# Weighted sum's strips and small loads issued in the stage before, and its preparations on VectorE put between the strips

## The chip, the cores and the metric

One core of a Trainium2 chip runs the whole program in a single launch. The metric is device time in microseconds, the median of several runs; the lower the better. The kernel before takes 2534.42 us (three runs, 2531.26 to 2535.39).

## What is computed

A chain of graph layers over 3125 nodes with 96 features and 50000 edges that are sorted by target, each wrapped as `layernorm(x + layer(x))`:

```python
x = _layernorm(x + _L0_gnn_ref(x, edge_index))        # 16 steps of normalised neighbour sums
x = _layernorm(x + _L1_gnn_ref(x, W0, b0, ..., src, dst))   # 2 layers: neighbour sum, weights, x / std
x = _layernorm(x + _L2_gnn_ref(x, edge_index, edge_weight)) # weighted neighbour sum
x = _layernorm(x + _L3_gnn_ref(x, edge_index, edge_attr_32, ...)) # 2 convolutions with a maximum over edges

def _L2_gnn_ref(X, edge_index, edge_weight):
    dst, src = (edge_index[0], edge_index[1])
    messages = edge_weight[:, None] * X[src]
    out = jax.ops.segment_sum(messages, dst, num_segments=X.shape[0])
    return out
```

## The kernel before

The nodes are padded to 25 blocks of 128 (`NB` = 25, `NP` = 3200), and a node block is a tile of 128 x 96. The program runs seven stages in a row, each a block of five instruction streams with a barrier of all engines behind it (`stage`): `prepare` and `build_counts` make a 3200 x 3200 matrix of edge counts `at` in float16 in SBUF; `appnp` multiplies by it 16 times and meanwhile GpSimd adds the edge weights into a matrix in HBM (`weight_matrix`, `d.mt`); `sage` does two more products by the counts with small weights and norms; `weighted_sum` is the third layer; `edge_conv` runs twice.

`weighted_sum` (tag `l2`) is the stage around which the change is made. The weight matrix has 25 strips, one for each block of targets; a strip is 128 x 27 x 128 float32, 1728 KB, of which 25 blocks meet node blocks and 2 meet "carried" rows: rows of `x` that a partition shares with another and that are fetched by two indirect DMAs on GpSimd (`far`) from a copy of `x` in HBM (`d.xt`, `x_table`). A matmul takes float16, so each strip and `x` are split into a high and a low part. In the kernel before, the engines' queues are these, in the order written:

- SyncE: strip 0, the store of `x` to `x_table` (lines 1196 and 1198), then strips 1 to 24. There are four places for strips (`STRIPS_IN`), so strip `o` waits until the low half of strip `o - 4` is made by VectorE (and by GpSimd, from `POOL_FROM` = 1 on).
- ScalarE: 17 small loads (targets, sources by tile, weights, biases, sources; lines 1349 to 1357), the high parts of `x` (1359), then for each strip its high half (1368); behind strip 0's, the high part of the carried rows (1371); a root behind strip 3's.
- GpSimd: waits for `x_table`, two gathers of the carried rows (1212), then the low half of the last 6 of 27 blocks (`BY_POOL`) of each strip from 1 on (1220).
- VectorE: the low parts of `x` (1231), the sources by tile (1298, 1299), the squares of the weights (`square_weights`), what depends on the targets (`edge_ends`, 1248 to 1265), the carried rows' low part, and then for each strip its low half (1310), with `bound_scales` behind strip 2, the carry row and `stream_of` behind 3, two scales behind 4, `stream_of` behind 5, and each five strips' sums, norm and table parts.
- TensorE: for each strip 54 matmuls with the high half and 54 with the low one (1395), into one half of a bank; strip 0's first pass waits group by group for the low parts of `x`, the last group being the carried rows. Behind strip 0 come the column norms (1413, 1414), behind strip 2 the carry row (1419).

The stage before it, `sage`, ends with the last group of five blocks: ScalarE's root (`square_root`, 157), VectorE's deviation and second norm (980 to 1041), a second root, and the last product with the inverse root into `m.x` (1060). Four other groups of that last norm are finished by ScalarE (947). SyncE has only the loads of the layer's weights there, at the start; GpSimd has one reduction over the partitions between the two layers. In `appnp`, VectorE starts with the scaled `dinv` (728), from which the first parts are made.

## Time and profile before

| what | value |
|---|---|
| median of 3 runs | 2534.42 us |
| the profiled execution's own time | 2547.56 us |
| its span, first to last instruction | 2545.8 us |
| TensorE matmul / VectorE / ScalarE / GpSimd busy | 81% / 67% / 36% / 49% of the span |
| `weighted_sum` from and to (us of the span) | 1368.8 to 1541.0 |
| last big product of `sage` ends; first gather of `edge_conv` issued | 1350.4; 1555.76 |
| mean granted clock of TensorE | 0.905 of full speed |

The profile is one execution. Times in the trace count from its first instruction. Shares of busy time are means over seven stages with different limits, so a reading for one stage takes the timeline of each engine in it, the waits with what ended them, and a table of busy time by stretch. In a timeline, "[idle before <- releaser]" is the time that the engine stood before the instruction and what ended it; neighbours of the same kind are merged ("x50" is fifty of them, from the start of the first to the end of the last). SP is SyncE, PE TensorE, DVE VectorE, ACT ScalarE, POOL GpSimd; "SPq", "ACTq" are DMAs that those engines issue.

### The profile page before, as it was taken

The page shows a single profiled execution, that of the slowest core. Times are in us where ns is not written, and L with a number is a line of the kernel's source. Part 1 is how long each engine was busy: PE and PEld are TensorE (multiplying, and loading weights), DVE is VectorE, ACT ScalarE, POOL GpSimd, SP SyncE. Part 2 cuts the span into 40 slices and gives each one's busy share as a digit, 9 for nine tenths or more (in the row PEclk, how much of TensorE's full clock was granted, in tenths as well). Part 3 has the DMA queues.
Part 4 walks back from the last instruction along what each step waited for, and adds up shares of the span by engine and source line. Part 5 has one row for each costly group of instructions (what it writes and reads, how often), then busy time and mean ns, then how long its engine had stood idle before and what let it go on. Part 6 is the DMA issues. An engine that isn't in the chain of part 4 may idle for free. (4 is left out here: it accounts for less than half of the span.)

```text
span 2545.8 us, 59620 instructions
## 1 busy us (share of the span) xinstructions
PE 2058.7 (81%) x23672; PEld 1897.4 (75%) x23672; DVE 1715.1 (67%) x4704; ACT 913.5 (36%) x1320; POOL 1249.8 (49%) x1021
## 2 busy tenths in 40 slices
PE   4494569999999999997983897888887578888860
PEld 4242259999999999997883896777776567778760
DVE  8999985555555555566555995767775356776656
ACT  0395520000000000001344555766773156777620
POOL 0200048878787778750001543666665246666651
PEclk9995579999999999998996997999998589999975
DMA  3593013232323232220004862344333034334321
GB/s 131 166 408 139 1 15 30 21 30 21 30 21 27 24 30 21 21 30 14 2 2 166 319 264 72 121 131 133 113 114 116 16 98 136 115 119 130 126 75 27
DMA packets 150636, 227.45 MB, mean 89 GB/s; under 512 B 87617, under 2 KB 109793, under 8 KB 147074
## 3 DMA queue, kind: packets, MB, share of 16 engines
q1 hardware_dynamic: 70418, 186.31, 20.2%
q0 software_dynamic: 74688, 28.51, 11.6%
q10 hardware_dynamic: 5296, 9.47, 1.2%
q8 instruction: 152, 2.49, 0.4%
q14 instruction: 82, 0.67, 0.1%
HBM read 123.37 MB, written 100.84 MB: 88 GB/s over the span
## 5 line engine op out<-in xcount | busy, mean ns | idle before, releaser
L637 PE MATMUL ps<-parts,at 128*128 128x192 f16 x11250 | 942.8, 247 | 23.7 <-POOL at L669 13.8
L637 PEld LDWEIGHTS ps<-parts,at 128*128 128x128 f16 x11250 | 935.8, 98 | 25.3 <-issue 24.3
L1782 PE MATMUL ps<-yparts,source_onehots_c 128*128 128x192 f16 x7000 | 681.3, 251 | 119.4 <-issue 103.5
L1782 PEld LDWEIGHTS ps<-yparts,source_onehots_c 128*128 128x128 f16 x7000 | 581.5, 100 | 185.5 <-issue 166.7
L1574 POOL DMA_INDIRECT messages_c<-y_table,srci_sb x504 | 499.6, 991 | 384.5 <-PE ps L1782 140.1
L679 POOL DMA_INDIRECT weight_matrix<-w,place x392 | 608.4, 1552 | 157.7 <-issue 96.5
L767 DVE SCALAR_TENSOR_TENSOR t<-ps,coef,g 128x96 f32<-128x96 f32 x400 | 126.8, 317 | 245.3 <-PE ps L637 202.3
L707 ACT ACTIVATE ea_limbs<-ea_in,ea_scale 128x392 f16<-128x392 f32 x32 | 19.9, 621 | 742.7 <-DMA ea_in<-in_eaT 734.4
L1657 DVE TENSOR_SCALAR source_onehots_c<-sources_spread,shift 128x1280 f16<-128x1280 f16 x512 | 283.1, 563 | 0.3
L1602 ACT ACTIVATE source_gaps_c<-sources_spread,unshift 128x1280 f16<-128x1280 f16 x188 | 256.3, 1364 | 23.0 <-DVE source_onehots_c L1657 5.5
L1706 DVE SCALAR_TENSOR_TENSOR messages_c<-messages_c,brk 128x96 f32<-128x96 f32 x784 | 249.9, 319 | 17.3
L1605 ACT ACTIVATE source_onehots_c<-source_gaps_c 128x1280 f16<-128x1280 f16 x188 | 238.8, 1270 | 6.0
L627 PE MATMUL ps<-onekey,oneplace 128*128 128x200 f16 x784 | 154.9, 358 | 80.5 <-DVE oneplace L582 80.5
L627 PEld LDWEIGHTS ps<-onekey,oneplace 128*128 128x128 f16 x784 | 78.9, 122 | 156.4 <-DVE oneplace L582 108.0
L1685 DVE TENSOR_TENSOR messages_c<-messages_c,ps 128x480 f32<-128x480 f32 x112 | 67.0, 598 | 149.4 <-remote 126.4
L1614 ACT ACTIVATE picked_pairs_c<-ps 128x384 f32<-128x384 f32 x140 | 59.7, 490 | 239.3 <-PE ps L1809 220.1
L770 DVE SCALAR_TENSOR_TENSOR t<-ps,coef,t 128x96 f32<-128x96 f32 x400 | 127.3, 318 | 14.1
L777 DVE CAST parts<-t 128x96 f16<-128x96 f32 x375 | 93.9, 251 | 55.6 <-DVE t L770 1.5
L669 POOL TENSOR_TENSOR at<-at,ident 128x128 f16<-128x128 f16 x25 | 10.9, 477 | 244.8 <-issue 244.8
L1677 DVE TENSOR_TENSOR messages_c<-picked_pairs_c 128x192 f32<-128x192 f32 x140 | 49.3, 352 | 95.3 <-ACT picked_pairs_c L1614 65.1
L562 ACT ACTIVATE counts<-ps 128x400 f16<-128x400 f32 x196 | 85.9, 622 | 69.0 <-PE ps L627 65.1
L779 DVE TENSOR_TENSOR parts<-t,parts 128x96 f16<-128x96 f32 x375 | 97.8, 261 | 13.4 <-DVE parts L777 0.5
(385 smaller groups left out, 1869.0 us busy)
## 6 DMA issues: line engine op xcount, KB each, us to landing
weight_matrix<-blank SPq DMA_DIRECT2D x27, 1600.0 KB
weights<-weight_matrix SPq DMA_DIRECT2D x25, 1728.0 KB
run_max<-messages_c SPq DMA_DIRECT2D x28, 960.0 KB
ea_c<-edge_limbs SPq DMA_DIRECT2D x28, 896.0 KB
edge_limbs<-ea_limbs SPq DMA_DIRECT2D x128, 98.0 KB
run_max<-messages_c SPq DMA_DIRECT2D x28, 384.0 KB
sources_spread<-sources_by_tile ACTq DMA_DIRECT2D x26, 320.0 KB
messages_c<-y_table,srci_sb POOLq DMA_INDIRECT x504
```

The lines of the kernel that those rows point to most:

```text
L627: nc.tensor.matmul(m.ps[:, n % 8, 256 * (s % 2):256 * (s % 2) + KEYS], oneplace[:, q % RING, h, :, j], onekey[:, q % RING, h, :, j], start ...
L637: mm = nc.tensor.matmul(m.ps[:, bank, 0:2 * D], m.at[:, s, blk * P:(blk + 1) * P], parts[:, s, :], start=(s == 0), stop=(s == NB - 1))
L679: nc.gpsimd.indirect_dma_start(cells, bass.IndirectOffsetOnAxis(m.place[:, t:t + 1], 0), m.w[:, t:t + 1], None, compute_op=ALU.add).then_i ...
L767: nc.vector.scalar_tensor_tensor(t1[:, r % 2, :], m.ps[:, r % NBK, 0:D], coef[:, i:i + 1], g0[:, i, :], ALU.mult, ALU.add).then_inc(tmp1, 1)
L770: nc.vector.scalar_tensor_tensor(t2[:, r % 2, :], m.ps[:, r % NBK, D:2 * D], coef[:, i:i + 1], t1[:, r % 2, :], ALU.mult, ALU.add).then_in ...
L779: nc.vector.tensor_tensor(parts[:, nxt, i, D:2 * D], t2[:, r % 2, :], parts[:, nxt, i, 0:D], ALU.subtract).then_inc(ready, 1)
L1574: nc.gpsimd.indirect_dma_start(msg[:, k % 2, j, :], None, d.yt, bass.IndirectOffsetOnAxis(m.srci[:, k * TURN + j:k * TURN + j + 1], 0)).th ...
L1602: nc.scalar.activation(gap[:], srcb[:, k % 2, :, :].rearrange("p i e -> p (i e)"), ACT.Abs, bias=m.unshift[:, b:b + 1]).then_inc(gapd, 1)
L1605: nc.scalar.activation(hot[:, b, :], gap[:], ACT.Relu, bias=1.0, scale=-1.0).then_inc(hota, 1)
L1657: nc.vector.tensor_scalar(hot[:, b, :], srcb[:, k % 2, :, :].rearrange("p i e -> p (i e)"), m.shift[:, b:b + 1], None, ALU.is_equal).then_ ...
L1706: nc.vector.scalar_tensor_tensor(msg[:, k % 2, j, :], prev, m.brk[:, TURN * k + j:TURN * k + j + 1], msg[:, k % 2, j, :], ALU.add, ALU.max ...
L1782: return nc.tensor.matmul(m.ps[:, i // 2, at:at + 2 * D], hot[:, b, i * P:(i + 1) * P], parts[:, b, :], start=(b == 0 and i % 2 == 0), sto ...
```

## The change

The buffers of the strips (`m.strips`), of their high halves and of two small loads are now placed by hand over the counts matrix `at` (`placed`), which is free after the last big product of `sage`; so are all tensors of the later stages. With that:

- `sage`, SyncE: once the last product is done, issues strips 0 and 1, the small loads, and strip 2 (`AHEAD` = 3). ScalarE: behind the first root of the last group, stores the first 20 blocks of `x` to `x_table` and makes the high halves of strips 0 and 1; behind the second root, waits for the last norm on VectorE (`xn`) and stores the last 5 blocks. GpSimd adds `rowptr` and `deg` (`e_end`).
- `weighted_sum`, ScalarE: no loads; the high parts of `x`, the carried rows' high part, and high halves from strip 2 on; its root moves behind strip 4. GpSimd: gathers, then the low half of 6 blocks of every strip, 0 too. VectorE: strip 0's low half comes right behind the low parts of `x`; `square_weights` and the carried rows' low part behind strip 0; the sources by tile behind 1, `edge_ends` behind 2, and the four other preparations each one strip later than before. SyncE: strips from 3 on. TensorE: strip 0 runs the 25 node blocks with the high and then with the low half, and the carried rows' 2 blocks last; column norms behind strip 1, carry row behind strip 3.
- `build_counts`, GpSimd: makes the square of `dinv` and the scaled `dinv`, which VectorE made in `appnp`.

```diff
@@ build_counts, GpSimd
             nc.gpsimd.memset(m.at[:, :, NW * W:NP], 0.0).then_inc(cleared, 1)
+            nc.gpsimd.tensor_tensor(m.dinv2[:], m.dinv[:], m.dinv[:], ALU.mult).then_inc(squared, 1)
+            nc.gpsimd.tensor_tensor(m.dinvs[:], m.dinv[:], m.gs[:].to_broadcast([P, NB]), ALU.mult).then_inc(squared, 1)
             g.wait_ge(cleared, 1)
+            g.wait_ge(squared, 2)
@@ appnp, VectorE
-            do(nc.vector.tensor_scalar(dinvs[:], m.dinv[:], m.gs[:], None, ALU.mult))
...
-            do(nc.vector.tensor_tensor(coef[:], m.dinv[:], m.dinv[:], ALU.mult))
-            do(nc.vector.tensor_scalar(coef[:], coef[:], 1.0 - ALPHA, None, ALU.mult))
+            do(nc.vector.tensor_scalar(coef[:], m.dinv2[:], 1.0 - ALPHA, None, ALU.mult))
@@ sage, SyncE
             sp.wait_ge(wl, 14 * 16)
+            strips = d.mt.rearrange("(o p k c) -> p o k c", p=P, k=MB, c=P)
+            sp.wait_ge(prod, 2 * NB)
+            for o in range(2):
+                sp.dma_start(m.strips[:, o, :, :], strips[:, o, :, :]).then_inc(m.fetched[o], 16)
+            sp.dma_start(m.srcti[:], d.src_t.rearrange("t e -> (t e)").rearrange("(p c) -> p c", p=P)).then_inc(m.stl, 16)
+            sp.dma_start(m.dsti[:], d.dst_s).then_inc(m.eld, 16)
+            for k in range(2):
+                sp.dma_start(m.wmr[:, k, 0:D], d.Wmsg[k]).then_inc(m.wld, 16)
+                sp.dma_start(m.wmr[:, k, D:2 * D], d.Wroot[k]).then_inc(m.wld, 16)
+                for l in range(LIMBS):
+                    sp.dma_start(m.we[l * DE:(l + 1) * DE, k, :], d.Wedge[k]).then_inc(m.wld, 16)
+                sp.dma_start(m.bias[:, k, :], d.bias[k].rearrange("(a f) -> a f", a=1).to_broadcast([P, D])).then_inc(m.wld, 16)
+            sp.dma_start(m.srci[:], d.src_s).then_inc(m.wld, 16)
+            for o in range(2, AHEAD):
+                sp.dma_start(m.strips[:, o, :, :], strips[:, o, :, :]).then_inc(m.fetched[o], 16)
@@ sage, GpSimd
             nc.gpsimd.partition_all_reduce(ga[:], gm[:], P, RMAX).then_inc(amx, 1)
+            nc.gpsimd.tensor_tensor(m.e_end[:], m.rowptr[:], m.deg[:], ALU.add).then_inc(past, 1)
+            g.wait_ge(past, 1)
@@ sage, ScalarE
+            def strip_high(o):
+
+                a.wait_ge(m.fetched[o], 16)
+                nc.scalar.activation(m.whi[:, o, :, :], m.strips[:, o, :, :], ACT.Copy).then_inc(m.high, 1)
+
+            def store_x(g, z):
+
+                if z < NEND:
+                    a.wait_ge(xs, z)
+                else:
+                    a.wait_ge(xn, 1)
+                rows = slice(g * ENDS, z * ENDS)
+                a.dma_start(d.xt.rearrange("(i p) f -> p i f", p=P)[:, rows, :], m.x[:, rows, :]).then_inc(m.xst, 16)
...
                         square_root(nc, a, m, roots + (g if layer == 0 else 2 * g) + 1, m.st2[:], ends(g))
+                        if layer == 1:
+                            store_x(0, g)
+                            strip_high(0)
+                            strip_high(1)
...
                         square_root(nc, a, m, roots + 2 * g + 2, m.st2[:], ends(g))
+                        store_x(g, NEND)
@@ weighted_sum, SyncE
-            for o in range(NB):
+            for o in range(AHEAD, NB):
                 if o >= STRIPS_IN:
                     sp.wait_ge(low_v, o - STRIPS_IN + 1)
-                    if o - STRIPS_IN >= POOL_FROM:
-                        sp.wait_ge(low_g, o - STRIPS_IN - POOL_FROM + 1)
+                    sp.wait_ge(low_g, o - STRIPS_IN + 1)
                 sp.dma_start(mt[:, o % STRIPS_IN, :, :], strips[:, o, :, :]).then_inc(fetched[o % STRIPS_IN], 16)
-                if o == 0:
-                    sp.dma_start(d.xt.rearrange("(i p) f -> p i f", p=P), m.x[:]).then_inc(xst, 16)
@@ weighted_sum, GpSimd
+            g.wait_ge(xst, 32)
             for q in range(PARTS):
                 nc.gpsimd.indirect_dma_start(far[:, q, :], None, d.xt,
                                              bass.IndirectOffsetOnAxis(m.carried[:, q:q + 1], 0)).then_inc(farg, 16)
+            for o in range(NB):
+                low_half(o)
             g.wait_ge(farg, 16 * PARTS)
@@ weighted_sum, VectorE
             for g in range(NEND):
                 low_parts(g)
-            v.wait_ge(stl, 16)
-            do(nc.vector.tensor_copy(srcf[:], srcti[:]))
-            nc.vector.tensor_scalar(srct[:], srcf[:], -float(MID), None, ALU.add).then_inc(stm, 1)
-            square_weights()
-            edge_ends()
-            low_parts(NEND)
...
+                if o == 0:
+                    square_weights()
+                    low_parts(NEND)
+                if o == 1:
+                    v.wait_ge(stl, 16)
+                    do(nc.vector.tensor_copy(srcf[:], srcti[:]))
+                    nc.vector.tensor_scalar(srct[:], srcf[:], -float(MID), None, ALU.add).then_inc(stm, 1)
                 if o == 2:
+                    edge_ends()
+                if o == 3:
                     bound_scales()
@@ weighted_sum, ScalarE
-            a.dma_start(dsti[:], d.dst_s).then_inc(eld, 16)
...
-            a.dma_start(m.srci[:], d.src_s).then_inc(wl, 16)
             for g in range(NEND):
                 nc.scalar.activation(xp[:, blocks(g), 0:D], m.x[:, blocks(g), :], ACT.Copy, scale=XSCALE).then_inc(xhigh, 1)
-            for o in range(NB + rows_at + 1):
+            a.wait_ge(farg, 16 * PARTS)
+            nc.scalar.activation(xp[:, NB:MB, 0:D], far[:], ACT.Copy, scale=XSCALE).then_inc(xhigh, 1)
+            for o in range(2, NB + rows_at + 1):
@@ weighted_sum, TensorE
+                if o == 0:
+                    sum_blocks(o, whi, nodes, True, False)
+                    low_made(o)
+                    sum_blocks(o, wlo, nodes, False, False)
+                    pe.wait_ge(xlow, NEND + 1)
+                    sum_blocks(o, whi, carried, False, False).then_inc(highs_used, 1)
+                    sum_blocks(o, wlo, carried, False, True).then_inc(summed, 1)
```

## Rows read from the trace of the kernel before

**Rows 1.** The timeline of VectorE around the stage boundary at 1368.8 us.

```profile
1367.07 0.66 DVE L1060 TENSOR_TENSOR x_sb<-y_sb,st 128x480 f32<-128x480 f32 x1
1378.61 2.93 DVE L1231 SCALAR_TENSOR_TENSOR x_parts<-x_sb,x_parts 128x480 f16<-128x480 f32 x5 [10.88 <-ACT x_parts L1359]
...
1381.84 0.37 DVE L1299 TENSOR_SCALAR srct<-srcf 128x392 f16<-128x392 f32 x1
...
1383.78 0.35 DVE L1248 CAST dstf<-dsti 128x392 f32<-128x392 int32 x1
...
1386.64 0.18 DVE L1259 TENSOR_TENSOR e_end<-rowptr,deg 128x25 f32<-128x25 f32 x1
...
1387.99 0.18 DVE L1265 TENSOR_SCALAR unshift<-shift 128x25 f32<-128x25 f32 x1
1391.83 0.36 DVE L1231 SCALAR_TENSOR_TENSOR x_parts<-carried_x,x_parts 128x192 f16<-128x192 f32 x1 [3.66 <-ACT x_parts L1371]
...
1435.69 0.70 DVE L1330 SCALAR_TENSOR_TENSOR y_sb<-ps,weight_unscale,x_sb 128x480 f32<-128x480 f32 x1
```

**Rows 2.** The timeline of ScalarE in the same stretch.

```profile
1359.97 0.21 ACT L157 ACTIVATE sd<-st 128x5 f32<-128x5 f32 x1 [2.31 <-DVE st L985]
1365.80 0.21 ACT L157 ACTIVATE sd<-st 128x5 f32<-128x5 f32 x1 [5.62 <-DVE st L1041]
1368.81 0.39 ACTq L1349 DMA_DIRECT2D dsti<-in_dst_s  x1
...
1377.97 2.58 ACT L1359 ACTIVATE x_parts<-x_sb 128x480 f16<-128x480 f32 x5 [11.96 <-issue]
...
1391.36 0.36 ACT L1371 ACTIVATE x_parts<-carried_x 128x192 f16<-128x192 f32 x1 [7.84 <-DMA carried_x<-x_table,carried]
...
1425.61 3.08 ACT L1368 ACTIVATE weights_high<-weights 128x3456 f16<-128x3456 f32 x1 [3.84 <-DMA weights<-weight_matrix]
```

**Rows 3.** The timeline of TensorE in the same stretch.

```profile
1383.57 4.18 PE L1395 MATMUL ps<-x_parts,weights_high 128*128 128x96 f16 x50 [27.90 <-ACT weights_high L1368]
...
1401.05 2.47 PE L1395 MATMUL ps<-x_parts,weights_high 128*128 128x96 f16 x54
...
1443.31 4.04 PE L1395 MATMUL ps<-x_parts,weights_low 128*128 128x96 f16 x54 [2.45 <-DVE weights_low L1310]
```

**Rows 4.** The timeline of GpSimd, the first gather of the carried rows.

```profile
1383.67 1.25 POOL L1212 DMA_INDIRECT carried_x<-x_table,carried  x1 [109.80 <-DMA x_table<-x_sb]
```

**Rows 5.** Busy time by stretch: length, PE, PEld, DVE, ACT, POOL, PEclk, DMA share, GB/s.

```profile
1401.00:1420.00 19.00, 18.00 (x415) 17.80 (x415) 17.95 (x32) 10.49 (x5) 11.45 (x5) 1.00 0.85 306
1440.00:1460.00 20.00, 17.19 (x357) 16.88 (x353) 19.58 (x13) 12.36 (x6) 10.37 (x3) 0.91 0.91 342
```

**Rows 6.** Durations by line: count, then ns at least/median/most.

```profile
L1310 DVE TENSOR_TENSOR weights_low<-weights,weights_high x25: 2943/2957/4404, 1392.1 to 1521.7; 128x2688 f16<-128x2688 f32 x24, 128x3456 f16<-128x3456 f32 x1
...
L1574 POOL DMA_INDIRECT messages_c<-y_table,srci_sb x504: 938/946/1579, 1555.8 to 2447.2; - x168
```

**Rows 7.** The timeline of VectorE at the head of `appnp`.

```profile
340.52 0.24 DVE L728 TENSOR_SCALAR dinv_scaled<-dinv,g_scale 128x25 f32<-128x25 f32 x1 [0.76 <-PEq L101]
```

**Rows 8.** The timeline of SyncE, two strips' issues (start, duration).

```profile
1369.66 10.28 SPq L1196 DMA_DIRECT2D weights<-weight_matrix  x1
...
1418.52 0.32 SPq L1196 DMA_DIRECT2D weights<-weight_matrix  x1
```

**Rows 9.** DMA issues at the span's end; us from issue to landing.

```profile
out<-x_sb SPq DMA_DIRECT2D x5, 240.0 KB, 2.3
```

**Rows 10.** DMA queues from 1372.0 to 1375.5 us: packets, MB, share of 16 engines.

```profile
q1 hardware_dynamic: 84, 1.13, 86.2%
q10 hardware_dynamic: 87, 0.14, 10.7%
```

**Rows 11.** Bytes moved from 1555.5 to 1562 us in 40 slices.

```profile
GB/s 32 0 0 0 0 0 0 0 0 0 0 0 0 19 151 132 0 0 0 0 0 0 95 208 0 0 0 0 0 0 189 114 0 0 0 0 0 0 227 76
```

**Rows 12.** Groups of VectorE by line and shape, 1392 to 1530 us.

```profile
L1310 DVE TENSOR_TENSOR weights_low<-weights,weights_high 128x3456 f16<-128x3456 f32 x1 | 3.8, 3752 | 0.0
```

156 lines of the change are left out of this document (85 added, 71 removed).

## The prediction

> **What bounds the kernel now.** I read the change first and asked which stages it touches: the end of layer two of `sage` (its last norms), the whole of `weighted_sum`, and two small operations at the head of `appnp`. So the page's shares for the whole span say little here; I went to the engine timelines on both sides of the stage boundary at 1368.8 us, and then to the table of stretches. In the boundary the reader should see this order: VectorE ends the last norm at 1367.07+0.66 = 1367.73 us [rows 1]; the next stage's first instruction comes 1.08 us later, and it is ScalarE's list of 17 small loads, which holds ScalarE until 1377.97 [rows 2]. TensorE waits until 1383.57 for its first matmul, runs 50 of strip 0's in 4.18 us, and starts strip 1 only at 1401.05, where 54 take 2.47 [rows 3]. What it waits for in between are the carried rows: `x_table` is stored, gathered from 1383.67 on [rows 4], and ScalarE gets them at 1391.36 [rows 2]. That is the wait the change aims at.
>
> Then I asked which engine sets the pace once strips flow, because only that engine's lead can be kept. From 1401 to 1420 VectorE is busy 17.95 of 19.00 us, from 1440 to 1460 19.58 of 20.00; TensorE 18.00 and 17.19 [rows 5]. VectorE is the one without slack: a strip's low half takes it 2.96 us as a rule and up to 4.40 [rows 6], and norms and bounds stand between them in the same queue. So from 1392 to the end of the strips I read VectorE's queue as the path, and I measure the change at one point of that queue: the moment at which the carried rows' low part (line 1231, at 1391.83 [rows 1]) is made.
>
> **Part 1, the head of `appnp`.** VectorE loses `dinv_scaled`, 0.24 us with a 0.03 gap [rows 7], ahead of all that makes the first parts: 0.27 us gained. The square of `dinv` comes off the queue when TensorE already has parts to work on; I take nothing. GpSimd gets both in `build_counts`, where it has a single memset and then nothing to do until the stage ends: no cost, since no engine waits for them before the stage ends.
>
> **Part 2, the last norms.** SyncE issues strips 0 and 1, the 17 small loads and strip 2, from the last big product (about 1350.4) on. A list of 17 took ScalarE 9.16 us (1368.81 to 1377.97 [rows 2]), so SyncE is through by about 1361, before the norms are: it is no late comer at the boundary. A strip issued alone took from 1418.52 [rows 8] to 1425.61, where ScalarE had waited for it [rows 2]: 7.1 us. So strip 0 is there by 1357.6 and strip 1, about 4.5 behind, by 1362. ScalarE's first root of the last group ends at 1359.97+0.21 = 1360.18; then it issues the store of 20 blocks (0.4) and copies two strips, 3.08 each [rows 2]: 1366.75. Its second root stood at 1365.80 [rows 2] and is now 0.95 late; the chain on VectorE behind it ends at 1368.7. ScalarE then issues the store of the last five blocks, 0.43, which VectorE's end formerly didn't have to wait for. With the same 1.08 for the boundary, the next stage begins at 1370.2: **1.4 us are lost**, and everything below is counted from there.
>
> **Part 3, the first strips.** ScalarE starts at once with the high parts of `x` instead of its list. VectorE follows: five low parts end 3.57 us after ScalarE's start (1377.97 to 1378.61+2.93 [rows 1, 2]), then strip 0's low half 2.95, then the squares of the weights, about 1: it stands at the carried rows at 1377.7. Up to here nothing binds but VectorE itself.
>
> When are the carried rows there? Call their arrival F; before it was 1391.36. It is the time at which the second part of the store has landed plus the gather. The store: 240 KB alone took 2.3 us to landing [rows 9], which from 1368.7 gives 1371.0. But two queues share the DMA engines packet for packet: beside strip 0 the one queue had 84 packets and the other 87 in the same 3.5 us [rows 10], while the bytes were 1.13 against 0.14 MB. The store has 25 x 128 = 3200 short rows, a strip only 128 long ones, so beside strips the store nearly stands still. It gets on between strips 1 and 2 and after strip 2; if the rest isn't through when strip 3 (issued at 1370.2) comes, it ends behind it, at about 1370.2+7.1+0.8 = 1378.1. I take 1375.5, past the middle, since the row with two queues at once is nearer to the case than the store alone. The gather: from 1383.67 to 1391.36 it took 7.7 us under full DMA traffic [rows 2, 4]; in a quiet stretch the first bytes of one flow 2 us after its issue ([rows 11]: slices of 0.16 us from 1555.5 on, and the issue was at 1555.76), which with a second gather 1.55 behind and its landing is about 5. Behind strip 3 the engines are quiet, because strip 4 must wait for GpSimd's share of strip 0, which is queued behind the gathers: I take 6.4. **F = 1381.9**, between 1376.0 and 1385.8.
>
> So at this point VectorE's queue is 1391.36-1381.9 = 9.46 us early. What it must do behind the point has changed. Gone is strip 0's low half, 3.75 [rows 12]. Added are the two operations on the sources (the second at 1381.84 for 0.37 [rows 1], the two 0.75) and `edge_ends`, 1383.78 to 1388.17, 4.39, less 0.22 for its addition [rows 1]: in the kernel before all of this lay in the wait for the carried rows, cover that is gone. Net +1.17. GpSimd takes 6 of 27 blocks of strip 0 while VectorE is idle, so it costs nothing; strip 2's high half waits for F on ScalarE and is made by F+3.4, while VectorE wants it at F+4.5.
>
> Who is late next? TensorE: strip 1 can begin at about 1384.4 and it needs less than 4.9 us a strip (two halves of 2.47 that overlap [rows 3]), where the strips so far came at 5.6 (strip 1 at 1401.05, strip 8's low half at 1443.31 [rows 3]); it keeps its slack. Strips 4 on are issued as VectorE frees the buffers, 7.1 to landing against three strips' lead. So VectorE stays the bound, and at the end of the strips the lead is the same; the tail behind and both `edge_conv` are untouched.
>
> Sum: 9.46-1.17+0.27 = 8.56 us. The profiled execution took 2547.56 us (its span 2545.8), which would become 2539.0; it is 13.1 above the median of the runs, and no term is a share of the span, so I take the same off the median: 2534.42-8.56 = **2525.9**.
>
> **The rivals.**
> *TensorE's lead is kept whole (0.07).* It starts strip 1 at 1384.4 instead of 1401.05, 16.6 us; if VectorE's busy time holds slack, since some of its low halves last 4.40 instead of 2.96 us where it only waits for GpSimd [rows 6], the time is 2534.4-16.6-0.3 = 2517.5. Against: 19.58 of 20.00, and a wait inside an instruction is spent all the same.
> *The store is through before strip 3 (0.06).* F near 1377.7, where VectorE itself is the limit: 13.7-0.9 = 12.8, 2521.6.
> *The carried rows come late (0.15).* Store 1378.1 and the full 7.7: F = 1385.8, gain 4.7, 2529.7.
> *VectorE shuts GpSimd's gathers out (0.08).* GpSimd's additions do wait while VectorE has two operands in SBUF. If gathers did too, they would start when strip 0's low half ends, at 1376.7, not 1375.5: F = 1383.1, gain 7.4, 2527.0. Against: 504 gathers beside a busy VectorE took 938 to 1579 ns [rows 6]. The Trainium skill (SBUF — State Buffer, "SBUF: two separate sides") says that the pair of ports is an exclusive lock and that a DMA issued from GpSimd starves meanwhile, as its descriptors can't be written. By that rule it is this rival that holds; the trace so far doesn't bear it out for gathers, only for additions.
> *An issue blocks (0.08).* SyncE's strip behind the long store of `x_table` took 10.28 us to issue [rows 8]. If ScalarE's second store stands so behind its first, the boundary moves by some 6 us, and with it everything: about 2.5 gained, 2531.9.
> *Slower: TensorE's clock (0.06).* Between strips 2 and 3 there is now `edge_ends`, 4.4 us on VectorE beside the low half's 2.96, and the bounds follow strip by strip, so TensorE waits some 2.5 us in each of about five strips. After a wait of 2.45 us a half strip took 4.04 us, not 2.47 (at 1443.31 [rows 3]; the granted clock is 0.91 in that stretch and 1.00 in 1401 to 1420 [rows 5], so it was at the lower level, 1.2 GHz, for part of it). A strip with both halves so costs some 8.1 us against the pace of 5.6: 2.5 lost each. The mechanism decides from 6 strips on, since 8.6+5.1 us must go; with nine, 22.5 are lost and the time is 2548. Against: a TensorE that is late has no waits, and the clock came back each time it was busy throughout.
>
> **How the numbers follow.** The forecast has 0.50. What a measurement of this kernel can tell from no change is about 0.2%, 5.1 us, so faster means below 2529.35. Faster: nearly all of the forecast, the first two rivals, most of the shut-out gathers and a third of the late rows: 0.73. Same: most of the late rows, the blocked issue: 0.20. Slower: the clock and a remainder, 0.07. The range takes in F from 1376 to 1385.8 and the blocked issue, and stops short of the whole of TensorE's lead: 2519.5 to 2532.5; outside it are about 0.06 below and 0.08 above.
>
> **What the changed profile would show.** Next stage's first instruction near 1370.2; ScalarE's second root of the last group near 1366.8; the carried rows' copy on ScalarE near 1381.9 with VectorE waiting for it since 1377.7; strip 1 on TensorE near 1384.4; the first sums of five strips on VectorE (1435.7 before) near 1427.5. If the carried rows are early and those sums aren't, VectorE's queue grew more than I counted. If the sums are earlier by over 12 us, VectorE was not the bound. If the boundary is later than 1372, an issue or a strip stood in ScalarE's way.

## The result

The changed kernel takes 2524.07 us (median of 5 runs, 2521.57 to 2525.85) against 2533.16 of the kernel before in the same series: ratio 0.9969, 95% interval 0.9958 to 0.9980, so 5 to 11 us faster. The forecast was 2525.9 with 73% on faster. The number is right, but it is the sum of three terms of which none was forecast with its size: a loss of 7.1 us was taken for nothing, and two gains were put too low. That the sum came out is luck. (In the first series of experiments below every run, those of before too, took near 2350 us instead of 2530, all of it in `edge_conv`, so a kernel is compared only by its ratio to the runs of before in its own series.) The ledger of the two profiled executions (before's took 2547.56 us, after's 2525.85, span 2524.1):

| stretch | forecast | measured |
|---|---|---|
| `build_counts`, to VectorE's last memset: 339.61 before, 346.75 after | 0 | +7.1 |
| from there to the last matmul of `sage`: 1015.5, then 1013.7 | -0.3 | -1.8 |
| from there to VectorE's first operation of `edge_conv`: 186.6, then 174.1 | -8.3 | -12.4 |
| sum up to `edge_conv` | -8.6 | -7.1 |

Behind that, `edge_conv` is the same work in both; that it was 14.6 us shorter in this execution is not the change's, as the medians differ by 9.1 us in all. The 2 us between these 9.1 and the 7.1 of the ledger are within the interval; the tiles of `edge_conv` lie elsewhere now, and whether that does anything stays open.

**Build.** Busy time by stretch (length, PE, PEld, DVE, ACT, POOL, PEclk, DMA share, GB/s), before and then after, while the weight matrix is cleared:

```profile
110.00:160.00 50.00, 50.00 (x263) 24.47 (x262) 50.00 (x67) 50.00 (x132) 0.00 (x0) 1.00 1.03 408
```

```profile
110.00:160.00 50.00, 50.00 (x262) 24.33 (x260) 50.00 (x67) 50.00 (x131) 49.65 (x1) 1.00 1.02 385
```

GpSimd is "busy" for the whole stretch with one 128x25 operation: it stood 53.60 us, beside VectorE's one-hots, which follow each other without a gap (they still did when it ended, so what let it in is not shown). More to the point, the clearing moves 385 GB/s, not 408, and so lasts until about 219 us, not 212 (by the bytes of the stretch from 200 to 220 us). VectorE's additions behind the one-hots stop where registers are loaded, and longer while the clearing runs; these waits in the build (waited for: us, times, longest), before and after, and the loads of registers from 180 to 210 us (ns at least/median/most):

```profile
DVE at L606 <- issue: 6.0, 13, 1.0
...
L600 DVEq TENSOR_LOAD <-off_sb x8: 1117/1136/1439, 179.9 to 204.1; - x8
```

```profile
DVE at L624 <- issue: 12.0, 13, 2.6
...
L618 DVEq TENSOR_LOAD <-off_sb x8: 1983/2007/2219, 179.8 to 209.5; - x8
```

The median load takes 1.13 to 1.15 us there in all nine traces with the quick clearing and 1.97 to 2.01 in all five with the slow one; behind the clearing it takes 0.60 in each.

**Head of `appnp`.** GpSimd's 25 additions and TensorE's first matmuls, before:

```profile
347.73 10.94 POOL L669 TENSOR_TENSOR at<-at,ident 128x128 f16<-128x128 f16 x25 [244.82 <-issue]
348.25 11.92 PE L637 MATMUL ps<-parts,at 128*128 128x192 f16 x123 [13.78 <-POOL at L669]
```

and after, where the stage begins at 347.65:

```profile
347.64 15.10 POOL L687 TENSOR_TENSOR at<-at,ident 128x128 f16<-128x128 f16 x25 [182.75 <-POOLq L101]
350.32 0.96 PE L655 MATMUL ps<-parts,at 128*128 128x192 f16 x5 [8.71 <-DVE parts L754]
```

Before, GpSimd's first addition comes 7.2 us behind VectorE's first operation; now both begin at once, share, and TensorE's first matmul comes 2.7 us into the stage, not 7.7. What GpSimd waited for is in its sequencer's rows, of before and then of after:

```profile
L669 POOLq MODIFY_POOL_CONFIG  x2: 11/11/11, 340.6 to 340.6; - x2
```

```profile
L553 POOLq MODIFY_POOL_CONFIG  x2: 12/12/12, 102.7 to 102.8; - x2
110.36 53.60 POOL L553 TENSOR_TENSOR dinv_squared<-dinv 128x25 f32<-128x25 f32 x1 [7.63 <-issue]
```

GpSimd's configuration is changed ahead of the first operation on two tensors (`TENSOR_TENSOR`) that follows its reduction over the partitions, and in all 14 traces that operation begins 6.9 to 7.6 us after this first change. In before the change of configuration stands at the head of `appnp`, where TensorE waits for it. With the two operations in the build, it is paid there, where nothing waits for GpSimd.

**Boundary.** ScalarE of after (start, duration; compare [rows 2]):

```profile
1364.83 0.21 ACT L172 ACTIVATE sd<-st 128x5 f32<-128x5 f32 x1 [2.31 <-DVE st L1038]
1364.84 0.44 ACTq L945 DMA_DIRECT2D x_table<-x_sb  x1
1365.32 6.06 ACT L936 ACTIVATE weights_high<-weights 128x3456 f16<-128x3456 f32 x2 [0.28 <-issue]
1371.29 0.19 ACT L172 ACTIVATE sd<-st 128x5 f32<-128x5 f32 x1
1373.29 0.37 ACTq L945 DMA_DIRECT2D x_table<-x_sb  x1
1374.70 2.58 ACT L1403 ACTIVATE x_parts<-x_sb 128x480 f16<-128x480 f32 x5 [3.22 <-PEq L101]
1385.04 0.36 ACT L1405 ACTIVATE x_parts<-carried_x 128x192 f16<-128x192 f32 x1 [7.76 <-DMA carried_x<-x_table,carried]
```

VectorE and GpSimd of after (compare [rows 1, 4]):

```profile
1378.19 2.95 DVE L1354 TENSOR_TENSOR weights_low<-weights,weights_high 128x2688 f16<-128x2688 f32 x1
...
1385.43 1.50 DVE L1283 SCALAR_TENSOR_TENSOR x_parts<-carried_x,x_parts 128x192 f16<-128x192 f32 x1 [3.44 <-ACT x_parts L1405]
1386.86 2.95 DVE L1354 TENSOR_TENSOR weights_low<-weights,weights_high 128x2688 f16<-128x2688 f32 x1
1389.72 1.81 DVE L1361 CAST srcf<-srcti 128x392 f32<-128x392 int32 x1
...
1428.87 0.71 DVE L1383 SCALAR_TENSOR_TENSOR y_sb<-ps,weight_unscale,x_sb 128x480 f32<-128x480 f32 x1
```

```profile
1379.19 3.01 POOL L1269 DMA_INDIRECT carried_x<-x_table,carried  x1 [93.61 <-DMA x_table<-x_sb]
1382.50 0.95 POOL L1269 DMA_INDIRECT carried_x<-x_table,carried  x1 [0.30 <-issue]
```

The first gather took 3.01 us, not 1.25, and it ends 1.06 behind VectorE's low half (1381.14): it was held for as long as that ran. TensorE of after (compare [rows 3]):

```profile
1376.14 4.16 PE L1436 MATMUL ps<-x_parts,weights_high 128*128 128x96 f16 x50 [15.07 <-DVE x_parts L1283]
1385.26 3.74 PE L1436 MATMUL ps<-x_parts,weights_low 128*128 128x96 f16 x50 [4.96 <-POOL weights_low L1264]
...
1389.17 2.46 PE L1436 MATMUL ps<-x_parts,weights_high 128*128 128x96 f16 x54
...
1404.18 3.41 PE L1436 MATMUL ps<-x_parts,weights_low 128*128 128x96 f16 x54 [2.20 <-DVE weights_low L1354]
```

From the last matmul of `sage` on (1355.09 before, 1360.43 after), the stage begins 14.2 us later instead of 13.7, the carried rows' low part comes at 25.0 instead of 36.7, the first sums of five strips at 68.4 instead of 80.6, `edge_conv` at 174.1 instead of 186.6. All that is gained is there by the first sums.

### The profile page after: what moved, and what is told of

Its sections match the earlier page's. It is cut to its first block and busy times, and to the rows that moved or that the text cites. A ratio compares the mean times of both kernels' runs of the same rounds, so it can differ in the third digit from the quotient of the medians.

```text
span 2524.1 us, 59625 instructions
## 1 busy us (share of the span) xinstructions
PE 2057.6 (82%) x23672; PEld 1883.9 (75%) x23672; DVE 1708.9 (68%) x4701; ACT 914.6 (36%) x1320; POOL 1308.8 (52%) x1025
## 5 line engine op out<-in xcount | busy, mean ns | idle before, releaser
L1835 PEld LDWEIGHTS ps<-yparts,source_onehots_c 128*128 128x128 f16 x7000 | 566.1, 98 | 189.9 <-issue 165.2
L687 POOL TENSOR_TENSOR at<-at,ident 128x128 f16<-128x128 f16 x25 | 15.1, 640 | 182.7 <-POOLq L101 182.7
L795 DVE TENSOR_TENSOR parts<-t,parts 128x96 f16<-128x96 f32 x375 | 97.2, 259 | 13.4 <-DVE parts L793 0.5
```

Of the source, the lines that this page charges most:

```text
L795: nc.vector.tensor_tensor(parts[:, nxt, i, D:2 * D], t2[:, r % 2, :], parts[:, nxt, i, 0:D], ALU.subtract).then_inc(ready, 1)
L1835: return nc.tensor.matmul(m.ps[:, i // 2, at:at + 2 * D], hot[:, b, i * P:(i + 1) * P], parts[:, b, :], start=(b == 0 and i % 2 == 0), sto ...
```

## The experiments

Twelve kernels, in three series of four. Each series has its own runs of the kernel before beside it, and only ratios to those are compared. The two stages around the change are alike in all series. The table reads the traces: GB/s of the clearing (110 to 160 us) and the build's last memset; then, in us from ScalarE's first copy in `weighted_sum`, the first gather and how long its issue took, the carried rows on ScalarE, their low part on VectorE, and the first sums; then the us from the last matmul of `sage` to the first operation of `edge_conv`.

| kernel | GB/s | build ends | gather (us) | rows | low part | sums | to `edge_conv` | ratio |
|---|---|---|---|---|---|---|---|---|
| before | 408 | 339.6 | 5.7 (1.25) | 13.4 | 13.9 | 57.7 | 186.6 | 1 |
| after | 385 | 346.8 | 4.5 (3.01) | 10.3 | 10.7 | 54.2 | 174.1 | 0.9969 |
| `build_alone` | 409 | 339.4 | 6.9 (1.19) | 14.2 | 14.7 | 58.7 | 187.6 | 0.9998 |
| `build_undone` | 385 | 346.3 | 4.5 (3.04) | 10.3 | 10.7 | 54.2 | 174.2 | 0.9977 |
| `ends_in_wait` | 385 | 346.7 | 4.6 (3.10) | 10.6 | 16.9 | 54.5 | 173.9 | 0.9963 |
| `store_first` | 385 | 346.6 | 4.5 (2.96) | 11.9 | 12.3 | 54.6 | 174.6 | 0.9967 |
| `before_blank` | 385 | 346.8 | 5.8 (1.20) | 13.8 | 14.3 | 58.2 | 188.3 | 1.0027 |
| `blank_moved` | 409 | 339.6 | 4.5 (3.05) | 10.4 | 10.8 | 54.2 | 174.4 | 0.9934 |
| `ends_first` | 408 | 339.3 | 4.7 (1.19) | 8.9 | 17.0 | 54.3 | 173.4 | 0.9941 |
| `vector_alone` | 409 | 339.6 | 6.0 (2.26) | 14.9 | 15.3 | 56.8 | 174.4 | 0.9943 |
| `alone_ends` | 408 | 339.6 | 8.9 (1.19) | 14.7 | 15.1 | 52.8 | 170.9 | 0.9931 |
| `rows_first` | 409 | 339.5 | 7.2 (2.26) | 12.6 | 13.0 | 49.6 | 167.2 | 0.9922 |
| `store_whole` | 409 | 339.4 | 10.8 (1.19) | 14.8 | 15.2 | 58.7 | 176.8 | 0.9953 |
| `strips_back` | 408 | 339.6 | 1.2 (1.19) | 10.4 | 17.1 | 59.9 | 179.6 | 0.9967 |

(In before, `build_alone` and `before_blank` that first copy stands behind 9 us of loads, so their columns in between start later.) The intervals of the ratios are 0.0010 to 0.0014 to each side.

**`build_alone`**: the first part of the change alone, made in the kernel before.

```diff
 # before, build_counts, GpSimd
+            nc.gpsimd.tensor_tensor(m.dinv2[:], m.dinv[:], m.dinv[:], ALU.mult).then_inc(squared, 1)
+            nc.gpsimd.tensor_tensor(m.dinvs[:], m.dinv[:], m.gs[:].to_broadcast([P, NB]), ALU.mult).then_inc(squared, 1)
```

> The kernel before with GpSimd's two additions in the build alone (the square of dinv and dinv_scaled on GpSimd in build_counts, both off VectorE in appnp). Nothing is left out. In the profile of after, the build ended 7.1 us later than in that of before (346.75 against 339.61), GpSimd's 128x25 operation stood for 53.60 us, and the zeroing of the weight matrix moved 385 GB/s, not 409. Theory (the operations cost nothing, the 7.1 us are the zeroing's rate in that one execution): this kernel takes 2532.9, the time of before less 0.3, and its build is long or short as its own zeroing is slow (385) or quick (409). Rival (GpSimd's held operation disturbs the zeroing or VectorE): +7, 2540, with about 385 GB/s and a build of 245 us between its first and last memset.

Ratio 0.9998 (0.9988 to 1.0008), with GpSimd's operation as long as in after and the clearing at full rate:

```profile
110.00:160.00 50.00, 50.00 (x263) 24.33 (x262) 50.00 (x67) 50.00 (x131) 50.00 (x1) 1.00 1.03 409
```

The held operation disturbs nothing. But the theory is only half right: it put the 7 us down to one slow execution.

**`build_undone`**: the same two operations taken out of the changed kernel.

```diff
 # after, build_counts, GpSimd
-            nc.gpsimd.tensor_tensor(m.dinv2[:], m.dinv[:], m.dinv[:], ALU.mult).then_inc(squared, 1)
-            nc.gpsimd.tensor_tensor(m.dinvs[:], m.dinv[:], m.gs[:].to_broadcast([P, NB]), ALU.mult).then_inc(squared, 1)
```

> The changed kernel with the two operations back on VectorE at the head of appnp, so that only the last norms and the first strips differ from before. Nothing is left out. Theory (they cost nothing in the build and give 0.3 at the head of appnp): 2524.4. Rival (the held operation costs 7 us in the build): 2517. What is then between this kernel and before is the worth of the strips' part alone: by the trace of after, from the last big product of sage to the first operation of edge_conv 174.1 us instead of 186.6, so 12.4 less, where the forecast had 8.3.

Ratio 0.9977 (0.9968 to 0.9985), 5.4 us of 2352. The build ended at 346.28 with 385 GB/s although the operations were gone. So the 7 us belong to the change and not to its GpSimd operations: something that all kernels made from after share. Its head of `appnp` is before's again, TensorE waiting for GpSimd's additions:

```profile
354.88 11.30 PE L652 MATMUL ps<-parts,at 128*128 128x192 f16 x102 [13.76 <-POOL at L684]
```

From the build's end to the last matmul of `sage` the three traces without the two operations on GpSimd take 1015.5, 1016.4 and 1017.0 us, the eleven with them 1013.6 to 1015.6, 1014.6 in the mean: about 1.7 us for the head, where 0.27 was forecast. It is all there at the end of `appnp`'s first product: VectorE's 25th combination of sums begins 62.0 to 63.1 us behind the build's last memset in the three, 59.7 to 61.1 in the eleven. Runs alone don't resolve it. Nor does a run take VectorE's 0.24 us away and leave GpSimd's change of configuration where it was; but that change, at 347.2 here, and the 7.1 us behind it are all of GpSimd's wait.

**`ends_in_wait`**: what VectorE does behind strips 1 and 2 put into its wait for the carried rows.

```diff
 # weighted_sum, VectorE, o == 0
                     square_weights()
+                    (the two operations on the sources)
+                    edge_ends()
                     low_parts(NEND)
```

> The changed kernel with the two operations on the sources and edge_ends in front of the carried rows' low part instead of behind strips 1 and 2. Nothing is left out. In the trace of after VectorE waits 3.44 us there for the carried rows and is busy without a gap from 1385.43 to 1443.31. Theory (VectorE's queue is the bound of the first strips): the wait is filled, the first sums of five strips come 3.4 us nearer to the stage's start (54.2 us after ScalarE's first copy in after, then 50.8), the time falls by 3.4 to 2520.7. Rival (TensorE or the transfers set the pace of the first strips): the sums stay at 54.2, 2524.1. Third (VectorE's work shuts GpSimd's gathers out: in after the first of them took 3.01 us and ended as VectorE's low half of strip 0 did): the carried rows come up to 5 us later and the time is that of after or up to 2 more.

Ratio 0.9963 (0.9951 to 0.9976); the sums came at 54.5, as the second and third theories had it, and neither's reason is in the trace. The rows came at 10.6, so nothing shut them out for longer; TensorE had waits left. VectorE lost the gain itself:

```profile
1385.77 3.94 DVE L1302 TENSOR_TENSOR brk<-dstf 128x391 f32<-128x391 f32 x1
...
1391.10 1.62 DVE L1311 TENSOR_SCALAR row_ends<-row_ends 128x25 f32<-128x25 f32 x1
```

These take 0.57 and 0.17 us when nothing is beside them. GpSimd's low halves of strips 0 and 1 ran from 1386.04 to 1389.28.

**`store_first`**: strip 3 asked for behind the store.

```diff
 # weighted_sum, SyncE, ahead of strip 3
+                if o == AHEAD:
+                    sp.wait_ge(xst, 32)
```

> The changed kernel with strip 3 asked for only when both parts of the store of x_table have landed. Nothing is left out. Theory (strip and store share the DMA engines packet for packet, so strip 3 at 1374.67 holds up the store issued at 1373.29, which had landed by 1379.2): the store lands 2.3 to 3 us after its issue, the gathers are issued before VectorE's low half of strip 0 begins (3.5 us after the stage's start), the carried rows are on ScalarE near 6.5 us after the stage's start instead of 10.3, VectorE's wait of 3.44 us is gone, 2520.7. Rival (what holds the carried rows is VectorE's low half, which shuts the gathers out, and the store was through in time): carried rows and time as in after, 2524.1; strip 3 comes 1 to 2 us later for nothing.

Ratio 0.9967 (0.9955 to 0.9979). The store took no less time to land: the second part was issued at 1375.02 and SyncE went on at 1380.78, 5.8 us later, where 5.6 had gone in after with strip 3 beside it. What the store waits for is strip 2. Packets by queue (q1 SyncE's strips, q10 ScalarE's store) from 1373 to 1377 us, while strip 2 moves, and from 1377 to 1381:

```profile
q1 hardware_dynamic: 150, 1.60, 94.0%
q10 hardware_dynamic: 277, 0.11, 9.5%
...
q10 hardware_dynamic: 1347, 0.51, 46.9%
q1 hardware_dynamic: 26, 0.14, 8.3%
```

So the theory's mechanism holds, with the wrong strip; and strip 3, now beside the gathers, brought the rows 1.6 us later (11.9), which moved the sums by 0.4.

**`before_blank`** and **`blank_moved`**: what do all kernels made from after share? Three new tiles (`row_ends`, `dinv_squared`, `dinv_scaled`), each taking 128 bytes per partition, are allocated ahead of all that follows, so `blank`, the source of the clearing, begins at byte 202176 instead of 201792. (`build_alone` has two of them: 202048.) Both kernels are made by the same two lines, in before and in after:

```diff
 # build_counts
+        sb("pad_ahead", [P, 32], F32)
         blank = sb("blank", [P, NP // 4], F32)
+        sb("pad_behind", [P, 32], F32)
```

> The kernel before with 128 unused bytes per partition in front of blank (the zeros from which the weight matrix is cleared in the build) and 128 behind it. blank then begins at byte 201920 of each partition, not 201792; the other tiles of the build move by 256. Nothing is left out. Seen so far: the clearing moved 409 GB/s in before and build_alone (blank at 201792 and 202048, both 64 bytes past a multiple of 256) and 385 in after and the three kernels made from it (202176, 192 past one), and the build was 7 us longer in these, with or without GpSimd's two operations. Theory (where blank begins sets the rate): 385 GB/s, the build's last memset near 346.5 instead of 339.5, 7 us slower than before, ratio 1.003. Rival (something else of the change, such as where other tiles or the program's instructions lie): 409 GB/s and the time of before.

> The changed kernel with the same 128 bytes in front of blank and 128 behind it: blank begins at 202304, 64 past a multiple of 256 as in before. Nothing is left out. Theory: 409 GB/s, the build ends near 339.5, 7 us less than after; on a chip where after stands to before as 0.997, this stands as 0.994. Rival: 385 GB/s and the ratio of after, 0.997.

Ratios 1.0027 (1.0016 to 1.0039) and 0.9934 (0.9921 to 0.9948): 128 unused bytes ahead of `blank` (and 128 behind, which keep the later tiles in step) make before 7 us slower and the changed kernel some 9 faster, 7 by the trace. `before_blank` and then `blank_moved`:

```profile
110.00:160.00 50.00, 50.00 (x263) 24.49 (x262) 50.00 (x67) 50.00 (x132) 0.00 (x0) 1.00 1.02 385
```

```profile
110.00:160.00 50.00, 50.00 (x263) 24.46 (x262) 50.00 (x67) 50.00 (x132) 50.00 (x1) 1.00 1.03 409
```

The starts 201792, 202048 and 202304, each 64 bytes past a multiple of 256, gave 408 or 409 GB/s in every trace; 201920 and 202176, each 192 past one, gave 385. The Trainium skill (DMA: Bandwidth & Descriptors, "How a descriptor splits into AXI transactions") says that a descriptor is cut at multiples of 256 bytes and that a first piece is fetched from the boundary below its start. In the trace of before the clearing's packets have the 3200 bytes that `blank` has per partition (6572 packets with 20.38 MB from 110 to 160 us, 204 of them tiny). By that account the good start needs 13 pieces and the bad one 14, which gives an estimate of 0.93 for the ratio of the rates; counted in the beats of 32 bytes that the same section has, the unused ones included, it is 102 against 106, or 0.96. The traces have 0.94, between the two, so they agree in kind and don't tell which count sets the rate. A start on a multiple of 256 would need 13 pieces too; no run tried it.

**`ends_first`**: on `blank_moved`, the moved work even further ahead.

```diff
 # weighted_sum, VectorE
             for g in range(NEND):
                 low_parts(g)
+            (the two operations on the sources)
+            edge_ends()
             stepped = 0
```

> blank_moved with the two operations on the sources and edge_ends behind the low parts of x and in front of strip 0's low half, not behind strips 1 and 2. Nothing is left out. Where these stood in the wait behind strip 0's low half (ends_in_wait), GpSimd's low halves came at the same time: edge_ends took 9.0 us instead of 6.4 and the first sums were not earlier. Theory (VectorE's queue is the bound, and the gathers are shut out only by long operations on two operands): here nothing of GpSimd's is due beside edge_ends, so it takes 4.4 us, the gathers are issued in 1.25 and 0.95 us, the carried rows' low part comes 1.6 us later than in after and 8.6 us are gone behind it: first sums 7 us, less a stall or two of 1.2, nearer to the stage's start than in after (54.2), about 48.4; time 5 to 6 below blank_moved. Rival (TensorE or the strips' transfers set the pace once VectorE is early): first sums at 52 or later, time within 2 of blank_moved.

Ratio 0.9941 (0.9927 to 0.9954). What it says of the gathers holds: with no long operation on VectorE beside them they took 1.19 and 0.95, and the rows came at 8.9 instead of 10.4.

```profile
1372.58 1.19 POOL L1271 DMA_INDIRECT carried_x<-x_table,carried  x1 [93.58 <-DMA x_table<-x_sb]
1374.07 0.95 POOL L1271 DMA_INDIRECT carried_x<-x_table,carried  x1 [0.30 <-issue]
1375.04 3.23 POOL L1266 TENSOR_TENSOR weights_low<-weights,weights_high 128x768 f16<-128x768 f32 x2
```

But "nothing of GpSimd's is due beside `edge_ends`" was wrong, since early gathers let GpSimd go on to its low halves at 1375.04, and one operation of 0.27 us stood for both of them:

```profile
1374.74 3.61 DVE L1311 TENSOR_SCALAR mrep<-ones,mcol 128x96 f32<-128x96 f32 x1
```

The sums stayed at 54.3: from ScalarE's first copy on VectorE was idle for 4.3 us instead of 6.4, and held for 10.1 instead of 7.9 (what its operations took beyond the least that the same ones take in these traces).

**`vector_alone`**: is it GpSimd's low halves that hold VectorE?

```diff
-BY_POOL, AHEAD = 6, 3
+BY_POOL, AHEAD = 0, 3
```

(with GpSimd's low halves and the waits for them gone)

> blank_moved with the low halves of all 27 blocks on VectorE and none on GpSimd. Nothing is left out. One of 27 blocks took VectorE 3.75 us in before, one of 21 takes 2.95. Theory (a low half on GpSimd holds VectorE's two-operand work up, and the operations of 0.15 to 0.4 us that took 1.3 to 1.8 are such holds: 19 us in all behind the carried rows in after): 25 x 0.8 = 20 us are added and 19 saved, the time stays within 3 us of blank_moved, and no small operation on VectorE is stretched. Rival (GpSimd's share is free): 20 us slower than blank_moved.

Ratio 0.9943 (0.9929 to 0.9956), the time of `blank_moved` and far from 20 us slower. The holds are gone: seven low halves behind the carried rows took

```profile
L1345 DVE TENSOR_TENSOR weights_low<-weights,weights_high 128x3456 f16<-128x3456 f32 x7 | 26.3, 3756 | 0.1
```

and no small operation is stretched. So GpSimd's 6 of 27 blocks buy nothing here: a strip's share takes 0.8 us off VectorE and mostly costs it a hold of 1.2 to 1.5. What `vector_alone` lost again is in its wait for the carried rows, 7.22 us: strip 4, which no longer waits for GpSimd, was asked for between the gathers.

**`alone_ends`** and **`rows_first`**: the same two steps without GpSimd in the way.

```diff
 # vector_alone + ends_in_wait's edit; rows_first also, SyncE:
+                    if o == STRIPS_IN:
+                        sp.wait_ge(farg, 16 * PARTS)
```

> vector_alone (all low halves on VectorE) with the two operations on the sources and edge_ends in front of the carried rows' low part. Nothing is left out. In vector_alone VectorE waits 7.22 us for the carried rows and nothing of GpSimd's holds it; what is moved is 5.1 us. Theory (VectorE's queue is the bound of the first strips, and in ends_in_wait and ends_first it was GpSimd's low halves that ate the gain): the wait shrinks to 2.1, the first sums come 5.1 us nearer to ScalarE's first copy (56.8 in vector_alone, then 51.7), the time falls by 5 (0.2%) against vector_alone: ratio to before 0.992. Rival (TensorE or the transfers set the pace once VectorE is early): the sums come at 55 or later, ratio 0.994 as in blank_moved, ends_first and vector_alone.

> alone_ends with strip 4 asked for only when the carried rows have been gathered. Nothing is left out. In vector_alone SyncE asked for strip 4 as soon as VectorE had made strip 0's low half, between the two gathers, and the carried rows reached ScalarE 14.9 us after its first copy; in ends_first, without a strip beside the gathers, 8.9. Theory: the rows come 3 to 4 us earlier, at 11 to 12, VectorE's remaining wait of 2 us is gone, first sums near 50, ratio 0.991. Rival (the late strip 4 is missed later): sums as in alone_ends or later, TensorE waits for strip 4's high part.

The sums came at 52.8 (51.7 expected) and 49.6 (50 expected): now moved work does fill the wait. VectorE at the carried rows in `vector_alone` and in `rows_first`:

```profile
1383.57 0.36 DVE L1274 SCALAR_TENSOR_TENSOR x_parts<-carried_x,x_parts 128x192 f16<-128x192 f32 x1 [7.22 <-ACT x_parts L1396]
```

```profile
1382.14 0.36 DVE L1276 SCALAR_TENSOR_TENSOR x_parts<-carried_x,x_parts 128x192 f16<-128x192 f32 x1 [0.16 <-ACT x_parts L1396]
```

This settles that VectorE's queue is the bound of the first strips. Ratios 0.9931 (0.9918 to 0.9945) and 0.9922 (0.9909 to 0.9936): `rows_first`, 2512.97 us against 2531.87 of before, is the fastest kernel of all. Its trace is 7.2 us shorter than that of `blank_moved` up to `edge_conv`, the ratios differ by 3 us; the intervals allow for it, and whether some is lost in `edge_conv` stays open. So does why the store lands 1.5 to 4.4 us later in the three kernels without GpSimd's share (gather at 6.0, 8.9 and 7.2).

**`store_whole`** and **`strips_back`**: which part of the change gains? Both on `blank_moved`.

```diff
 # store_whole: sage, ScalarE
-                            store_x(0, g)
...
-                        store_x(g, NEND)
+                        store_x(0, NEND)
 # strips_back: no strip in sage
-BY_POOL, AHEAD = 6, 3
+BY_POOL, AHEAD = 6, 0
-                            strip_high(0)
-                            strip_high(1)
```

> blank_moved with x_table stored in one piece behind the last norm, not 20 blocks before the two strips' copies and 5 behind. Nothing is left out. The records of store_first show the 2560 short rows of the first part mixed one to one with strip 2's long ones and some 700 of them still waiting when strip 2 is through; the last of all leave near 1378.9, 1.9 before SyncE sees the landing. Theory (the carried rows' arrival hangs on the 3200 rows of the store): all 3200 rows now go beside strip 3, the gathers are issued 5 to 8 us later, VectorE's wait for the carried rows grows from 3.5 to 9 or 11, the first sums come 6 to 7 us later than in blank_moved (54.2), ratio 0.996. Rival (VectorE's queue has slack behind): the rows come late, the sums and the time don't, 0.9935.

> blank_moved with no strip asked for or copied in sage: strips 0 to 3 are asked for at the start of weighted_sum, strip 0's high half is made behind the high parts of x. The small loads and the store in two parts stay in sage. Nothing is left out. Theory (the gain is the carried rows', the strips ahead only fill the time until then): the second root of the last norms is 0.6 earlier, strip 0 lands 7.1 after the stage's start, its high half is made by 10.3 and its low half by 13.3, the carried rows follow at once, strip 1's low half begins near 14.5 instead of 12.2 after ScalarE's first copy, the time is 1 to 3 above blank_moved: ratio 0.9944. Rival (the strips ahead are what gained): 6 or more above it, 0.996 or higher.

`store_whole`: 0.9953 (0.9939 to 0.9966); gather 6.4 us later, rows 4.4, sums 4.5, the stage 2.4. The rows' arrival matters, but about half is made up by the end of the strips. `strips_back`: 0.9967 (0.9956 to 0.9979), and here the rival was right. With no strip in its way the store was through 0.9 us after ScalarE's first copy,

```profile
1368.87 1.19 POOL L1265 DMA_INDIRECT carried_x<-x_table,carried  x1 [89.35 <-DMA x_table<-x_sb]
```

yet VectorE then waited for the strip, and the squares behind it were held by GpSimd:

```profile
1378.18 2.96 DVE L1350 TENSOR_TENSOR weights_low<-weights,weights_high 128x2688 f16<-128x2688 f32 x1 [6.92 <-ACT weights_high L1401]
1381.06 1.80 DVE L1317 TENSOR_TENSOR weights_squared<-w_msg_root 96x192 f32<-96x192 f32 x1
```

Strip 1's low half began at 17.4, not 14.5. Of the 12.4 us, by the traces, the strips ahead carry 5.3 and the split of the store 2.4; each taken out alone; the rest goes with what both kernels keep, the list of loads and the store out of the stage and VectorE's preparations between the strips, and was not split further. By the runs the strips ahead are worth 8 us rather than 5.3 (0.9967 against 0.9934, each with about 3 us to each side).

## Why the prediction was right, point by point

**Build "no cost": wrong, for a reason that it didn't consider.** GpSimd's operations cost nothing (`build_alone`), but the tiles that the change adds move `blank` by 384 bytes, and the clearing's rate falls by 6%: 7.1 us. The step that failed is the reading of the change part by part, which counted instructions and no addresses. The forecast hit only because this loss met gains that it had put too low.

**Head of `appnp`: 0.27 forecast, about 1.7 measured.** The step that failed is that the two operations on GpSimd do nothing but move: they bring its change of configuration forward into the build, and GpSimd's additions, for which TensorE waits, start 7.2 us earlier.

**Last norms: 1.4 us forecast lost, 0.5 measured.** Counted from the last matmul of `sage`, the second root stood at 10.7 before and at 10.9 after, 0.15 late instead of 0.95, because the first root came 0.5 sooner there; VectorE's last product ended at 12.6 and 12.8. The boundary itself went from 1.08 to 1.50 with the store's issue in it, as forecast.

**VectorE at the carried rows 7.5 us into the stage: right** (7.3, at 1381.99). **Carried rows 11.7 us into the stage:** measured 10.4 (1385.04 from 1374.67). The store landed by 1379.15, 4.5 us in (5.3 forecast); the gather took 5.85 us (6.4 forecast) although the first was held for 1.8. The rule of the packets was right in kind: the store crawled beside a strip,

```profile
x_table<-x_sb ACTq DMA_DIRECT2D x1, 240.0 KB, 5.6
```

5.6 us against the 2.3 of [rows 9]. That it would share with strip 3 was not (`store_first`).

**The shut-out gathers, 0.08, were what happened,** in all seven traces in which the low half of strip 0 lay beside the first gather: 2.96 to 3.10 us in five, 2.26 in the two in which it came towards the end of that operation, and 1.19 to 1.25 in the other seven. (In `rows_first` it began only 0.08 us before that operation ended; the squares of the weights, on two tensors too, came next.) The trace of before had no such case: none of the 504 gathers of [rows 6] took over 1.58. The Trainium skill (SBUF — State Buffer, "SBUF: two separate sides") says that a DMA issued from GpSimd can't write its descriptors while VectorE has the shared pair of ports, and in these seven traces it is so. The price, 1.2 forecast, was 1.4 (10.4 against 8.9), but its removal gained nothing by itself (`ends_first`).

**+1.17 us behind the point: wrong term, -0.4 measured** (43.86 us from the carried low part to the first sums before, 43.44 after). The gone 3.75 and the moved operations are there. What the sum lacked are the holds: most of GpSimd's low halves cost VectorE one or two of 0.6 to 1.5 us somewhere, 9.3 us in all in this stretch of before and 7.9 in after. In before they fell on the low halves, of which seven took

```profile
L1310 DVE TENSOR_TENSOR weights_low<-weights,weights_high 128x2688 f16<-128x2688 f32 x7 | 24.9, 3575 | 0.1
```

and in after on the moved operations (1389.72 above: 1.81 for 0.35), while the low halves ran free:

```profile
L1354 DVE TENSOR_TENSOR weights_low<-weights,weights_high 128x2688 f16<-128x2688 f32 x7 | 20.7, 2956 | 0.1
```

4.2 us less there, and 1.9 less on the bounds, pay for the moved work and for the holds that now fall on it. The prediction had seen the 4.40 of [rows 6] and took it for a wait spent in any case.

**GpSimd's share of strip 0 "costs nothing": not quite.** TensorE waited 4.96 us for it (row at 1385.26 above), and VectorE's low part of the carried rows took 1.50 us for 0.36 beside it. It came that early, right behind the gathers, only because GpSimd's change of configuration had been made before: in before it stands behind the gathers (1386.28; the first low half came at 1395.96), in after in `sage`, ahead of the small sum of `rowptr` and `deg` (1277.8, the sum 7.5 us later). The prediction counted that sum as 0.22 us off VectorE.

**VectorE is the bound: right.** It has no wait over 0.2 us from 1385.43 to 1443.31 in after, and `alone_ends` and `rows_first` show the queue answering almost one to one. Strip 1 on TensorE came 14.5 us into the stage (14.2 forecast), the first sums at 54.2 (57.3 forecast).

**The clock: two half strips, not six strips.** In after (stretches as in [rows 5]) it was at 0.91 of full speed from 1394 to 1413, so for part of the time at the lower level, behind a wait of 2.20 us on TensorE. It was there again from about 1429 on, behind one of 1.94, and then back at 1.00:

```profile
1394.00:1413.00 19.00, 16.80 (x332) 15.99 (x332) 17.78 (x38) 7.51 (x4) 5.69 (x3) 0.91 0.78 272
1430.00:1435.00 5.00, 5.00 (x91) 5.00 (x89) 4.83 (x7) 2.21 (x2) 0.45 (x1) 0.72 0.90 337
1433.00:1453.00 20.00, 18.40 (x423) 18.10 (x421) 19.26 (x11) 12.75 (x5) 9.31 (x4) 1.00 0.85 326
```

```profile
1429.01 4.07 PE L1436 MATMUL ps<-x_parts,weights_low 128*128 128x96 f16 x54 [1.94 <-DVE weights_low L1354]
```

In before it fell once in the flow of the strips, behind the 2.45 us of [rows 3]. So the rival's mechanism is there, at 0.9 and 1.6 us a half strip (3.41 and 4.07 for 2.47), but TensorE had slack to take it.

**The other rivals.** No issue of ScalarE's blocked (0.44 and 0.37). TensorE's lead was not kept whole: it starts strip 1 17.2 us earlier against the last matmul of `sage` (28.7 instead of 46.0), and 12.4 are left at the end.

## What to carry to other kernels

A tile added early moves every tile allocated behind it, so look at the rate of the large transfers in a stage that the change doesn't touch before believing that it cost nothing. When GpSimd goes over from a reduction to operations on two tensors, look for the change of its configuration and let it fall where nothing waits for GpSimd: here it was worth more than the operations moved. Where GpSimd and VectorE both work in SBUF on two operands, look at what each operation takes alone and beside the other before splitting work between them: handing GpSimd a share may gain nothing, and work moved into a wait fills it only if GpSimd has nothing to do in it. And a forecast that meets the time is not yet a right one; the ledger by stage found the 7 us that could be had back.

## What was not expected of the hardware

- Where in SBUF the source of a large transfer begins, modulo 256 bytes, is worth 6% of its rate: 408 or 409 GB/s at 64, 385 at 192.
- An operation on GpSimd of 128x25 elements stood for 53.60 us beside an unbroken stream of two-operand work on VectorE; the other way round, GpSimd's low halves of some 1.65 us hold even one-operand casts of VectorE (1.81 for 0.35 us).
- GpSimd's change of configuration (`MODIFY_POOL_CONFIG`), two instructions of some 0.01 to 0.08 us in the trace, is followed by 5.5 to 6.1 us ahead of the first reduction over the partitions and 6.7 to 7.6 us ahead of a `TENSOR_TENSOR` that waits for nothing else, in which GpSimd does nothing and the profile shows nothing that it waits for. It explains the 7.2 us at the head of `appnp`. The prediction's premise that GpSimd's additions wait for VectorE was not what the trace of before had there.
- VectorE's loads of registers took 2.0 us while the clearing ran at 385 GB/s, 1.14 at 408, and 0.60 with the clearing over; they made gaps of up to 2.6 and 1.0 us.
- In `edge_conv` TensorE's instructions can come late without anything that the profile shows them to wait for. The profile of before has (waited for: us, times, longest)

```profile
PE ps L1782 <- issue: 103.5, 200, 2.3
```

and the traces of the first series have no such wait. It is about half of the 197 us or so by which `edge_conv` differs between them. Why the instructions came late in one and not in the other, no run tells.
